# Dense expert retrieval on one core: choosing one block ahead, in two places, in place of two blocks ahead

## What is computed

```python
xn = _rmsnorm(x, norm_w)
q = (xn @ w_q.T).reshape(b, t, H, 2, DK)
sim1 = jnp.einsum('bthd,hkd->bthk', q[..., 0, :], keys[:, :, 0, :])
sim2 = jnp.einsum('bthd,hkd->bthk', q[..., 1, :], keys[:, :, 1, :])
s1, i1 = jax.lax.top_k(sim1, K)
s2, i2 = jax.lax.top_k(sim2, K)
all_sc = (s1[..., :, None] + s2[..., None, :]).reshape(b, t, H, K * K)
fs, pk = jax.lax.top_k(all_sc, K)
...
hidden = jax.nn.gelu(jnp.einsum('btd,bthkd->bthk', xn, wd), approximate=False)
hidden = hidden * jax.nn.relu(fs)
return jnp.einsum('bthk,bthkd->btd', hidden, wu)
```

## Time and profile before

| | us |
|---|---|
| median of 3 runs | 1616.66 |
| lowest, highest | 1616.08, 1621.06 |
| profiled execution: its own time | 1626.32 |
| profiled execution: its span | 1624.6 |
| busy in the span: PE | 1506.1 |
| busy in the span: DVE | 1065.0 |
| busy in the span: ACT | 457.8 |
| busy in the span: POOL | 461.6 |

### The profile page before, as it was taken

How to read it: one execution, slowest core, us unless ns; L and a number is a source line. 1 busy time by engine, 2 the same in 40 slices (tenths; PEclk the granted TensorE clock), 3 DMA queues, 4 the chain that set the end, 5 groups by cost and what they waited for, 6 DMA issues and landing times. The chain is left out here.

```text
span 1624.6 us, 26917 instructions
## 1 busy us (share of the span) xinstructions
PE 1506.1 (93%) x10648; PEld 920.3 (57%) x10648; DVE 1065.0 (66%) x3217; ACT 457.8 (28%) x727; POOL 461.6 (28%) x392
## 2 busy tenths in 40 slices
PE   7998789999999999899989999899999999999882
PEld 3447668888888887444334433344444457543861
DVE  1639988696969747388789677644783398613734
ACT  2333111111111100133233332321112477612344
POOL 0001422323232511356666766700000000000263
PEclk9999899999999999999989999999999999999985
DMA  8910000000000012386656775630142027000234
GB/s 354 239 22 1 2 2 8 2 8 3 8 3 8 3 35 80 123 286 202 185 168 185 253 221 172 188 134 0 52 156 65 12 74 241 25 7 0 75 127 110
DMA packets 91024, 155.93 MB, mean 96 GB/s; under 512 B 42523, under 2 KB 56980, under 8 KB 88852
## 3 DMA queue, kind: packets, MB, share of 16 engines
q1 hardware_dynamic: 68884, 82.91, 15.9%
q0 software_dynamic: 22016, 71.32, 14.8%
HBM read 141.62 MB, written 16.78 MB: 97 GB/s over the span
## 5 line engine op out<-in xcount | busy, mean ns | idle before, releaser
L521 PE MATMUL peer_ps_h<-all_x,layer_down 128*128 128x256 f32 x768 | 181.1, 390 | 0.2 <-issue 0.2
L659 POOL TENSOR_TENSOR peer_bm<-peer_bm,peer_slots 128x512 f32<-128x512 f32 x36 | 109.0, 3028 | 245.3 <-DVE peer_bm L755 245.3
L521 PEld LDWEIGHTS peer_ps_h<-all_x,layer_down 128*128 128x128 f32 x768 | 145.0, 193 | 22.2 <-issue 2.3
L560 PE MATMUL peer_ps_o<-peer_hg,layer_up 128*128 128x256 f32 x640 | 142.4, 381 | 1.1 <-DVE peer_hg L787 1.1
L604 ACT ACTIVATE peer_hg<-peer_ps_h 128x512 f32<-128x512 f32 x96 | 57.3, 597 | 272.3 <-PE peer_ps_h L521 272.3
L560 PEld LDWEIGHTS peer_ps_o<-peer_hg,layer_up 128*128 128x128 f32 x640 | 120.6, 190 | 21.0 <-issue 3.3
L1482 PE MATMUL skills_ps_u<-all_x,skills_w 128*128 128x512 f32 x256 | 122.6, 602 | 8.9 <-issue 4.8
L1444 PE MATMUL skills_acc<-skills_hid,skills_w 128*128 128x512 f32 x256 | 120.7, 595 | 7.5 <-issue 4.2
L1482 PE MATMUL skills_ps_g<-all_x,skills_w 128*128 128x512 f32 x256 | 120.4, 592 | 0.0
L1515 ACT ACTIVATE skills_act_g<-skills_ps_g 128x512 f32<-128x512 f32 x83 | 48.9, 596 | 211.1 <-PE skills_ps_g L1482 160.5
L819 POOL DMA_INDIRECT layer_qw<-expert_rows,all_route x88 | 88.2, 1002 | 50.9 <-issue 25.7
(11 more groups left out here) (459 smaller groups left out, 2626.9 us busy)
## 6 DMA issues: line engine op xcount, KB each, us to landing
four_ring<-in_l_w SPq DMA_DIRECT2D x8, 1024.0 KB, 4.9
quant_w<-in_l_w SPq DMA_DIRECT2D x32, 256.0 KB, 4.1
all_early<-in_l_w SPq DMA_DIRECT2D x26, 256.0 KB, 3.4
skills_w<-in_skills SPq DMA_DIRECT2D x16, 384.0 KB
layer_down<-in_down SPq DMA_DIRECT2D x1, 4096.0 KB, 26.0
layer_up<-in_up SPq DMA_DIRECT2D x1, 4096.0 KB, 35.8
expert_rows<-in_up SPq DMA_DIRECT2D x1, 4096.0 KB, 41.1
four_skill<-in_skills SPq DMA_DIRECT2D x1, 3072.0 KB
```

The costliest lines, as they stand in the source:

```text
L521: mm = pe.matmul(ps_h[group % 2][:, r, :], down[:, c, j * P:(j + 1) * P], g.x[:, c, bass.ds(i * PB, PB)], start=(c == 0), stop=(c == C - 1))
L560: mm = pe.matmul(ps_o[:, c, :], up[:, j, c * P:(c + 1) * P], hg[half][:, j, :], start=(j == 0), stop=(j == NJ - 1))
L659: pool.tensor_tensor(bm[c % RING][:], bm[c % RING][:], slots[half][:, 2, c * PAIRS:(c + 1) * PAIRS].unsqueeze(2).to_broadcast([P, PAIRS, WJ]),
```

## The change

In blocks 0 to 3, `pick(i + 1, 0)` is spread over the first four chunks of block i, two pieces per chunk, and `pick(i + 1, 1)` follows whole after the last chunk. In block 4 both tiles of block 5 are spread over the eight chunks (`both=True`). Nothing is chosen two blocks ahead any more. PE's scores and transposes and ACT's copies move with that: `scores(i + 1, 0)` follows the first `weigh`, `scores(i + 1, 1)` the last group (in block 4 the fifth `weigh`), `turn(i + 1, 0)` stands after group 9, and `turn(i + 1, 1)` inside the up product, after 48 of its 64 matmuls (in block 4 after 2). On ACT one function, `follow`, takes the place of `ahead` and of what stood there for block 1.

```diff
--- before.py
+++ after.py
@@ -537,34 +537,29 @@
                                            start=True, stop=True)
                 mm.then_inc(w_ready, 1)
 
-            def work(i, half, first=False, last=False, route=True):
-
+            def work(i, half, last=False):
+
+                second = (0, 2) if last else (1, NJ // 2)
                 for c in range(CHUNKS):
                     weigh(i, c)
-                    if first and c % CPT == 0:
+                    if c == 0 or last and c == CPT:
                         scores(i + 1, c // CPT)
                     for group in range(c * GPC, (c + 1) * GPC):
                         act_rows(i + 1, group)
-                        if first and group == NGRP // 2 + 1:
+                        if group == NGRP // 2 + 1:
                             turn(i + 1, 0)
-                        if not first and group == 2:
-                            turn(i + 1, 1)
-                if route:
-                    scores(i + 2, 0)
+                if not last:
+                    scores(i + 1, 1)
                 pe.wait_ge(p_done, i * CHUNKS + CHUNKS + 1)
                 pe.wait_ge(x_done, i)
                 for c in range(C):
                     for j in range(NJ):
+                        if (c, j) == second:
+                            turn(i + 1, 1)
                         if last and j % (C * NJ // CHUNKS) == 0:
                             weigh(i + 1, (c * NJ + j) * CHUNKS // (C * NJ))
                         mm = pe.matmul(ps_o[:, c, :], up[:, j, c * P:(c + 1) * P], hg[half][:, j, :],
                                        start=(j == 0), stop=(j == NJ - 1))
-                        if c == 0 and j == NJ // 2 and first:
-                            turn(i + 1, 1)
-                        if c == 0 and j == NJ // 2 and route:
-                            scores(i + 2, 1)
-                        if c == 1 and j == 2 and route:
-                            turn(i + 2, 0)
                 mm.then_inc(o_ready, 1)
 
             keep_running(pe, g, ps_t[:], 1)
@@ -576,12 +571,12 @@
                 if group == 5:
                     turn(0, 0)
             turn(0, 1)
-            work(0, 0, first=True)
+            work(0, 0)
             with pe.Fori(0, NPB // 2 - 2) as r:
                 work(r * 2 + 1, 1)
                 work(r * 2 + 2, 0)
             work(NPB - 3, 1)
-            work(NPB - 2, 0, last=True, route=False)
+            work(NPB - 2, 0, last=True)
             late_scores(0)
             pe.wait_ge(p_done, NPB * CHUNKS + 1)
             pe.wait_ge(x_done, NPB - 1)
@@ -616,18 +611,20 @@
                 act.wait_ge(a_done, (i - 1) * CHUNKS)
                 act.wait_ge(b_done, (i - 1) * CHUNKS)
 
-            def ahead(i, half, route=True):
-
-                slots_free(i)
-                keep(i, half, 0)
-                act.wait_ge(o_ready, i - 1)
+            def follow(i, half, reused=True, stage=True):
+
+                if reused:
+                    act.wait_ge(o_ready, i - 1)
                 for group in range(NGRP):
                     gelu(i, half, group)
-                    if group == 3:
-                        keep(i, half, 1)
-                    if group == NGRP // 2 and route:
-                        act.wait_ge(sim_ready, (i + 1) * PT)
-                        stage_x(i + 1)
+                    if group == NGRP // 2 + 1:
+                        if reused:
+                            slots_free(i)
+                        keep(i, half, 0)
+                if stage:
+                    act.wait_ge(sim_ready, (i + 1) * PT)
+                    stage_x(i + 1)
+                keep(i, half, 1)
 
             act.sem_inc(gelu_done, 1)
             stage_x(0)
@@ -638,19 +635,12 @@
             keep(0, 0, 1)
             act.wait_ge(sim_ready, PT)
             stage_x(1)
-            for group in range(NGRP):
-                gelu(1, 1, group)
-                if group == NGRP // 2 + 1:
-                    keep(1, 1, 0)
-                if group == NGRP // 2 + 3:
-                    act.wait_ge(sim_ready, 2 * PT)
-                    stage_x(2)
-            keep(1, 1, 1)
+            follow(1, 1, reused=False)
             with act.Fori(0, NPB // 2 - 2) as r:
-                ahead(r * 2 + 2, 0)
-                ahead(r * 2 + 3, 1)
-            ahead(NPB - 2, 0)
-            ahead(NPB - 1, 1, route=False)
+                follow(r * 2 + 2, 0)
+                follow(r * 2 + 3, 1)
+            follow(NPB - 2, 0)
+            follow(NPB - 1, 1, stage=False)
 
         @block.gpsimd
         def _(pool):
@@ -762,7 +752,7 @@
                 dve.wait_ge(o_ready, i + 1)
                 dve.tensor_tensor(g.x[:, :, bass.ds(i * PB, PB)], ps_o[:], xin[:], ALU.add).then_inc(x_done, 1)
 
-            def work(i, half, first=False, last=False, route=True):
+            def work(i, half, first=False, both=False, last=False):
 
                 for c in range(CHUNKS):
                     n = i * CHUNKS + c
@@ -772,9 +762,9 @@
                         build(i + at // CHUNKS, at % CHUNKS, (half + at // CHUNKS) % 2)
                     if c == 0 and not first and not last:
                         add_out(i - 1)
-                    if first:
-                        if c % CPT == 0:
-                            parts = pick(i + 1, c // CPT)
+                    if c % CPT == 0:
+                        parts = pick(i + 1, c // CPT)
+                    if (c < CPT or both) and not last:
                         for _ in range(GPC):
                             next(parts)
                     if c == 0:
@@ -785,10 +775,9 @@
                     z0, m0 = 2 * (c // CPT), c % CPT * PAIRS
                     acts = h[:, z0:z0 + 2, :, m0:m0 + PAIRS]
                     dve.tensor_tensor(acts, ps_w[:].rearrange("p z m j -> p z j m"), acts, ALU.mult).then_inc(p_done, 1)
-                if route:
-                    for t in range(PT):
-                        for _ in pick(i + 2, t):
-                            pass
+                if not both and not last:
+                    for _ in pick(i + 1, 1):
+                        pass
 
             dve.sem_inc(p_done, 1)
             for t in range(PT):
@@ -801,8 +790,8 @@
                 work(r * 2 + 1, 1)
                 work(r * 2 + 2, 0)
             work(NPB - 3, 1)
-            work(NPB - 2, 0, route=False)
-            work(NPB - 1, 1, last=True, route=False)
+            work(NPB - 2, 0, both=True)
+            work(NPB - 1, 1, last=True)
             add_out(NPB - 2)
             for t in range(2):
                 for _ in pick(NPB, t, late=True):
```

## The result

| | before | changed |
|---|---|---|
| median, us | 1618.43 (4 runs) | 1673.97 (4 runs) |
| lowest, highest | 1616.08, 1621.06 | 1670.08, 1680.67 |
| profiled execution: its own time | 1626.32 | 1680.67 |
| profiled execution: its span | 1624.6 | 1678.9 |
| mean granted clock of PE | 0.971 | 0.951 |

The changed kernel is slower by 3.46% (ratio 1.0346, 95% interval 1.0322 to 1.0370), that is by 55.5 us of medians. 48.6 was forecast, and the time of 1674 lies in the range of 1650 to 1680. The table of the kernel before has one run more (1620.21) than the prediction had. In a later series, where the kernel before took 1630.10, the changed kernel had a ratio of 1.0345 (1.0310 to 1.0379).

The account below looks back on a forecast made before the run. PE was taken to bound blocks 1 to 4 and DVE block 0. Terms of -14.3, +27.3 and +25.6 gave +38.6, with +10 for the clock 48.6; on 1616.7 that made 1665 us, range 1650 to 1680.

Parts of the forecast that it names:

- Blocks 1 to 4 are bound by PE, block 0 by DVE: Before the change, PE was busy for all of block 1's 80.2 us; block 0 took 111.9, with DVE busy for 99.1.
- +9.1 for each of blocks 1 to 3: First four chunks: PE waits 8.7 us for DVE's products, plus 0.4 for slots of the next build; +27.3 in all.
- +25.6 for block 4: Block 4's chunks gain both choices and both scores: 71.3 us against 45.7, at full clock.
- The second tile costs nothing: Up product: the second choice takes 15.80 us and ends before its transpose, at 20.9, so PE does not wait.
- the margin of 5.1: Up product: us between the second choice's end (15.80) and its transpose (20.9); any excess would go straight to PE.
- -14.3 for block 0: Losing block 2's choice saves 18.4 us, less a `weigh` stop of 2.39 and a slow stretch of 1.7, both uncovered.
- The clock, +10: Blocks 1 to 4: slow stretches behind five of six new waits over 4 us reach the path, 2.0 us each.
- the third case: Rival, chance 0.13: the clock falls behind every wait, short ones mostly hidden by DVE; +60 us, 1677.
- The upper bound of 3.4: Most that one slow stretch may cost, in us, from two slow 4 us windows behind block 0's wait of 4.30.
- The case of a clock that holds: Rival, chance 0.2: waits come as worked out, no slow stretch falls on the path; +38.6 us, 1655.
- The case of a clock that falls behind every wait: Rival, chance 0.13: slow stretches behind short waits cost some 4 us, the five visible ones 7 more; +60, 1677.
- The faster case: Rival, chance 0.03: DVE's spare time in the chunks takes up the pieces; block 4 adds only two scores; 1609.

Follow-up runs that it names:

- The kernel half a block further ahead: Against the kernel before, choosing one and a half blocks ahead, two choices beside each up product of blocks 1 to 3: 1620.21 against 1624.16, ratio 0.9979.
- the experiment and its correction: Changed kernel without block 5's choice in block 4: ratio 1.0228 to the kernel before; block 4's chunks 55.6 us, less 3.2 from a wait the test itself added.
- the filled short waits: Changed kernel with 2 matmuls of no use ahead of the third and fourth `weigh` of blocks 0 to 4: ratio 1.0339 to the kernel before.

## Why the prediction was right, point by point

- **Blocks 1 to 4 are bound by PE, block 0 by DVE.** Right: with the choice of block 2 gone, block 0 fell from 111.9 to 98.9 (97 to 98 forecast), and each of blocks 1 to 4, in whose chunks pieces now stand, became longer. The kernel half a block further ahead shows both at once.
- **+9.1 for each of blocks 1 to 3.** The waits are as worked out: 35.0 to 35.4 to the fifth `weigh` in the three (34.7), 0.47 before the seventh (0.4). With the pieces behind the product PE's waits for it fall from 44.1 to 22.1 over `peer`, so about half of them come from the place. One small wait was missing, 0.3 to 0.6 before the second `weigh`, since the maxima and a product end just behind PE's groups.
- **+25.6 for block 4.** The chunks took 77.4 against 71.3 worked out at full clock; 75 was forecast with the clock. Without the pieces they would have taken 52.4, by the experiment and its correction.
- **The second tile costs nothing.** Right, with the margin of 5.1: no wait in any up product, and 8.9 per block once the margin is overdrawn by 8.8.
- **-14.3 for block 0.** Measured -13.1. The stop inside the fifth `weigh` did come into the open, at 1.03 where 2.39 was taken. The slow stretch behind it was larger than the 1.7 taken: 10.7 from this `weigh` to the transpose, 1.0 of it the stop, where 5.56 is full clock, so about 4.1. The two errors cancel in part.
- **The clock, +10.** The size was about right, the rule behind it wrong. The step that failed is the reading that only a wait of over 4 us is followed by a slow stretch: in this trace waits of 1.9 to 2.2 were, too. The trace of the kernel before had spoken against it already, with slow stretches in block 0 behind a stop of 1.53 inside a `weigh`, and behind a wait of 1.13 with the stop of 2.39:

```profile
190.00:194.00 4.00, 3.42 (x32) 0.67 0.00 0
...
202.00:206.00 4.00, 4.00 (x33) 0.63 0.02 4
```

Behind the short waits it cost nothing, as the third case had worked out (a slowed chunk of 7.35 under DVE's own time), and the filled short waits agree with that. Behind the waits of 4.7, with 5.56 from that `weigh` to the transpose at full clock and the stops taken off, the slow stretch cost 1.5, 3.6 and 3.1 in blocks 1 to 3 of this profile, and 3.2, 2.9 and 0.3 in the second one: 8.2 and 6.4, where 6 had been taken. With what block 4's chunks took above 71.3 and the stop in its fifth `weigh` that makes 13.5 and 10.4 against 10. That it came so near owes something to luck, since single blocks lie anywhere from 0.3 to 3.6. The upper bound of 3.4 was also misread: its first window, 170 to 174, is idle for 2 us of the wait itself. From the `weigh` at 171.98 to the next at 180.25 PE took 8.27, so 2.6 was lost.
- **What was left out.** The stops with no semaphore inside `weigh` (1.69 in block 2, 0.71 in block 3, 0.83 in block 4) were counted for block 0 alone. The kernel before had none in blocks 1 to 4. These 3.2, the 1.3 of small waits, the 1.2 too much that block 0 was to give, the 1.2 behind block 4's chunks and the 3.5 of the clock above its term in this profile are most of what lies between the 48.6 forecast and the 59.7 that `peer` grew by; the other layers took 5.3 less in that execution. For the 55.5 between the medians no such account can be drawn up, since only profiled executions show their blocks.
- **The rivals.** The case of a clock that holds (+38.6) is out. The case of a clock that falls behind every wait (+60) came closest in mechanism, and the truth lies between it and the forecast; but the 4 us that it charges for the short waits did not come. It compared a slowed chunk with DVE's mean of 8.53, where the chunk in question takes 7.59 on DVE. A chunk of 8.81 even stood there in block 4 (553.98 to 562.79), and the fifth `weigh` still started 35.03 after the first: the next product stands behind the longest pieces, which leaves PE the time. The faster case stayed far off: DVE's spare time is 1.62 per chunk, and only with the pieces behind the product does it take up part of them.

The Trainium skill ("TensorE: Matmul & The Clock Gate", section "HAM oscillation — how this bites in real kernels") tells of a loop whose waits are long, and warns of idle gaps above a length; that it would hold for every wait was the prediction's extension of it. The trace agrees with the page for the waits of 4.7 (0.50 behind 4.70), and goes beyond it for the shorter ones, some of which were followed by a slow stretch (0.57 behind 1.91) and some not (1.00 behind 2.00).

## What to carry to other kernels

Before spreading an engine's side work into a tight loop, compare the piece with the engine's idle time per turn of that loop (here 4.5 against 1.62), and leave it beside the long stretch of the other engine if it fits there. Where it must go into the loop, put it behind the instruction that the other engine waits for: here the same pieces cost half as much there. Count a wait together with the slow stretch behind it only where the waiting engine is the bound afterwards; where it is, matmuls of no use in the wait can buy part of it back, if they do not themselves end late.

## What was not expected of the hardware

- The granted clock fell behind waits of 1.9 to 2.2 us inside a busy stretch (0.57 behind 1.91), and once behind 1.63, while waits of 2.04 and 2.13 before block 0 left it at 1.00, and so did waits of 2.00 and 1.76 in one block of another run, at the very place where it fell in the changed kernel. So the length of the wait alone does not decide. What does was not tried.
- Five matmuls of 0.86 us in a wait of 4.7 kept the clock at 1.00 behind that wait in all three blocks. In one of them it fell elsewhere, behind waits of 1.76 and 0.71.
- `weigh`, a run of 64 small matmuls, stopped in its middle for 0.2 to 2.4 us in all profiles, with no semaphore behind it: 5.1 us in the kernel before, 5.9 and 10.2 in two profiles of the changed one. It was not tested what it waits for. A hint: a packet of the profile's `instruction` DMA queue passed shortly before several of these stops (at 399.0 before the one that ends at 401.69 in the changed kernel, at 198.6 before the one that ends at 201.46 in the kernel before). Such packets also passed where PE did not stop (at 389), so it is no more than a hint.
